# A two-layer MoE with a mixer between, on one core: the slot table from one-hot products and row gathers per expert, in place of zeroed, scattered and reloaded rows

## The chip, the core and the metric

The kernel runs on one core of a Trainium2 chip. Times are device microseconds (us) of one execution. The core's engines are named as the profile names them: PE is TensorE's matmuls, PEld its weight loads, DVE VectorE, ACT ScalarE, POOL GpSimd, SP SyncE, which here only issues transfers. "Granted clock" is the share of TensorE's full clock that the chip allowed in a stretch.

## What is computed

The input x is 2 x 1024 tokens of 512 values, float32. Three stages each add to it: a sparse feed-forward layer with 8 experts, a mixer, and the same feed-forward layer again. Every stage works on the layer-normalized x.

```python
x = x + 0.5 * ffn(layernorm(x), gate_weight, wi, wo)
x = x + mixer(layernorm(x), Wu, bu, Wv, bv, Wg1, bg1, Wg2, bg2, conv_w, conv_b)
x = x + 0.5 * ffn(layernorm(x), gate_weight, wi, wo)

def ffn(inputs, gate_weight, wi, wo):          # T = 2048 tokens, E = 8, C = 320
    logits = tokens @ gate_weight.T
    probs = softmax(logits)
    top1 = argmax(logits)
    mask = one_hot(top1, E)
    ranks = cumsum(mask, axis=0) - 1
    mask = mask * (ranks < C)
    weight = mask * probs                       # at the chosen expert
    dispatch = einsum('tec,th->ech', sec_mask, tokens)
    hmid = gelu(einsum('ech,ehi->eci', dispatch, wi))      # wi 8 x 512 x 2048
    eout = einsum('eci,eih->ech', hmid, wo)                # wo 8 x 2048 x 512
    return einsum('tec,ech->th', combine_weights, eout)
```

So a token goes to its best expert only, in the order of the tokens, and the 321st and later tokens of an expert are dropped. The mixer is a depthwise convolution over three tokens, two projections u and v gated by a small two-step network, a running sum of u over a sequence, and a product with Wu's transpose.

## The kernel before

Tokens lie on SBUF's 128 partitions in 16 tiles, worked on in 4 groups of 4 tiles. Products of float32 are made as three products of rounded halves: a high and a low half of each operand (names ending in h and l), which gives lines L1062 to L1064 (first product of an expert) and L1069 to L1071 (second).

**Routing.** For each group: DVE takes mean and variance (L742 to L749), POOL the power -0.5 (L433) and the shift (L435), ACT normalizes four tiles (L527; of the first group DVE does two, L755), PE turns them (L1099), ACT copies the turned blocks (L537), and PE multiplies by the gate's columns, four accumulating matmuls with 8 columns of weights (L1114). DVE copies the 8x512 result (`lgT`, L772), PE turns it back (L1121), and `route` on DVE finds the best expert, its one-hot row and the exponentials' sum; PE counts the ranks with triangular and all-one matrices (L1134 to L1137). `route(g)` works on the choice of group g and on the ranks of group g-1 in one round of about 20 small operations. Its result is `to_row`, the row of each token in a table in HBM.

**The table `disp`.** It has 2560 slots of 516 values. SP writes zeros over it (L318, four transfers of 1287.5 KB), POOL writes each slot's own number into the last column (L461, 2560 elements of four bytes), and once a group's `to_row` is known and the zeros lie, POOL scatters the normalized tiles with weight, deviation, mean and token number as four further columns, one indirect transfer per tile (L456, 16 per layer). When all have landed, SP loads expert 0's slots (L332, L334) into `dtok`.

**An expert.** PE turns `dtok` (L1160), ACT and DVE split it into high and low half (L583, L734). `wi` and `wo` come in four 1 MB units each, loaded two ahead by SP, split by ACT (L565, L576) and DVE (L734). The hidden layer goes through gelu (L596). ACT restores the unnormalized rows `xr` from `dtok` (L624), DVE copies weight and token number (L922, L923), multiplies and adds (L939), and POOL scatters three parts of up to 128 rows to x1 or out (L506). SP loads `dtok` for the next expert after the turning.

**PE's program.** An expert is computed over the width that its number of tokens needs: 240, 256, 272, 288, 304 or 320 columns, each with its own body of instructions, aligned to blocks of 256. `dispatch` compares the number (loaded into a register by L1239, at each expert) with the widths and branches. It is used twice: `visit`, which branches to the last instruction of the body's block and back at once, ahead of the turning, and `run`, which goes to the body. PE, ACT, DVE and POOL run their expert loops as loops on the chip. Before its loop PE waits for the counts, for the pads that DVE wrote, and for the first split weights.

**Between.** After layer 1's experts SP reloads x1 as `xt`; the mixer runs group by group; the normalizing and routing of layer 2 begin among the mixer's last additions. Layer 2's routing then is the same as that of layer 1, without zeros.

The lines that a sentence can't say as well:

```python
for t in range(g * GROUP, (g + 1) * GROUP):
    pool.indirect_dma_start(disp[:, :], bass.IndirectOffsetOnAxis(ap=to_row[:, t:t + 1], axis=0),
                            xn[:, t, :], None).then_inc(s.scattered, 16)
...
sp.wait_ge(s.scattered, 16 * TILES)
sp.wait_ge(s.taken_done, 1)
load_tokens(s, 0)
...
pe.wait_ge(s.taken_done, 1)
pe.wait_ge(pad_set, n + 1)
pe.wait_ge(s.wi_lo, 1)
```

## Time and profile before

| | us |
|---|---|
| median of three runs | 1210.59 |
| the runs' range | 1208.7 to 1220.23 |
| the profiled execution | 1222.94 |
| its span, from first to last instruction | 1221.2 |
| mean granted clock in it | 0.945 |
| PE, DVE, ACT, POOL busy in it | 1069.9, 737.1, 566.7, 127.8 |

The rows further below are of the profiled execution. "x4" is a count of instructions; a duration before it is their sum, or, where they overlap, the time from the first's start to the last's end. In brackets stands how long the engine was idle before, and what ended that; "issue" is a wait for nothing that the profile shows. In the chain of waits a row is a piece of the path that ended last. In the rows of the page on transfers the last number is the median time from issue to landing.

### The profile page before, as it was taken

What the parts mean: (1) busy time and instruction counts of PE and PEld (TensorE: products, weight loads), DVE (VectorE), ACT (ScalarE), POOL (GpSimd) and SP (SyncE); (2) the same over time, 40 slices, a digit from 0 to 9 for tenths busy, and PEclk for the clock granted to TensorE, in tenths of its full rate; (3) what the DMA queues carried; (4) which work ended last, traced back from release to release, by engine and by line L of the source; (5) the groups of instructions that cost most, each with busy time, mean ns of one, the idle gap of its engine ahead of it and who ended that gap; (6) DMA issues with size and microseconds to landing.
All of it is one profiled execution on the core that took longest, in us unless ns stands there. A gap on an engine that the chain in (4) does not pass through costs nothing.

```text
span 1221.2 us, 20880 instructions
## 1 busy us (share of the span) xinstructions
PE 1069.9 (88%) x7658; PEld 989.6 (81%) x7659; DVE 737.1 (60%) x1199; ACT 566.7 (46%) x871; POOL 127.8 (10%) x140
## 2 busy tenths in 40 slices
PE   5469796999999999759999983999999999879895
PEld 2169795999999999747787751899999999879795
DVE  6535453666657667448777764456767677645551
ACT  4335342556555556344334232445556565534341
POOL 3500101010101101100000015001101001010100
PEclk9779898999999999979999996899999999979998
DMA  9775734375554854040000024644557547523420
GB/s 255 241 253 197 284 121 143 119 253 191 193 193 126 281 185 168 24 136 1 1 35 30 6 104 164 238 159 160 203 180 253 193 153 277 205 92 124 160 69 21
DMA packets 90332, 189.08 MB, mean 155 GB/s; under 512 B 4592, under 2 KB 5104, under 8 KB 90224
## 3 DMA queue, kind: packets, MB, share of 16 engines
q1 hardware_dynamic: 84272, 169.50, 41.2%
q0 software_dynamic: 6016, 18.97, 4.1%
q8 instruction: 31, 0.51, 0.2%
q14 instruction: 13, 0.11, 0.0%
HBM read 160.02 MB, written 32.62 MB: 158 GB/s over the span
## 4 chain that ended last, share of the span: by engine, by line
PE 75%; issue 7%; DMA 6%; ACT 4%; DVE 3%; POOL 3%; SPq 1%; DVEq 0%; ACTq 0%; POOLq 0%
PE psH L1062 11%; PE psH L1063 11%; PE psH L1064 11%; PE acc L1069 9%; PE acc L1070 9%; PE acc L1071 9%; DMA raw_wi<-in_wi 4%; PE acc L1062 3%; PE acc L1063 3%; PE acc L1064 3%; POOL disp L456 2%; PE acc L1160 1%; PE psT L1204 1%; PE psH L1160 1%; PE psT L1099 1%
## 5 line engine op out<-in xcount | busy, mean ns | idle before, releaser
L1062 PE MATMUL psH<-dth,wih 128*128 128x240 f32 (+5 forms) x1024 | 298.8, 292 | 11.3 <-issue 9.4
L1069 PE MATMUL acc<-hth,woh 128*128 128x240 f32 (+5 forms) x1024 | 293.9, 287 | 6.3 <-DVE htl L734 6.3
L1063 PE MATMUL psH<-dtl,wih 128*128 128x240 f32 (+5 forms) x1024 | 297.2, 290 | 0.0
L1064 PE MATMUL psH<-dth,wil 128*128 128x240 f32 (+5 forms) x1024 | 296.8, 290 | 0.0
L1070 PE MATMUL acc<-htl,woh 128*128 128x240 f32 (+5 forms) x1024 | 293.3, 286 | 0.0
L1071 PE MATMUL acc<-hth,wol 128*128 128x240 f32 (+5 forms) x1024 | 293.1, 286 | 0.0
L734 DVE TENSOR_TENSOR wol<-raw_wo,woh 128x1024 fp32r<-128x1024 f32 x128 | 156.4, 1223 | 134.4 <-ACT woh L576 134.3
L1062 PEld LDWEIGHTS psH<-dth,wih 128*128 128x128 f32 x1024 | 196.9, 192 | 15.1 <-issue 13.7
L596 ACT ACTIVATE gel<-psH 128x320 f32<-128x320 f32 x256 | 111.0, 437 | 202.3 <-PE psH L1064 199.1
L576 ACT ACTIVATE woh<-raw_wo 128x1024 fp32r<-128x1024 f32 x128 | 135.4, 1059 | 146.1 <-PE acc L1071 144.4
L1069 PEld LDWEIGHTS acc<-hth,woh 128*128 128x128 f32 x1024 | 193.0, 188 | 7.9 <-DVE htl L734 7.9
L1063 PEld LDWEIGHTS psH<-dtl,wih 128*128 128x128 f32 x1024 | 196.9, 192 | 0.0
L1064 PEld LDWEIGHTS psH<-dth,wil 128*128 128x128 f32 x1024 | 196.7, 192 | 0.0
L1070 PEld LDWEIGHTS acc<-htl,woh 128*128 128x128 f32 x1024 | 193.0, 189 | 0.0
L1071 PEld LDWEIGHTS acc<-hth,wol 128*128 128x128 f32 x1024 | 193.0, 188 | 0.0
L734 DVE TENSOR_TENSOR wil<-raw_wi,wih 128x1024 fp32r<-128x1024 f32 x128 | 155.8, 1219 | 14.3 <-ACT wih L565 14.3
L565 ACT ACTIVATE wih<-raw_wi 128x1024 fp32r<-128x1024 f32 x128 | 134.8, 1054 | 18.5 <-DMA raw_wi<-in_wi 18.5
L891 DVE CAST hth<-gel 128x640 fp32r<-128x640 f32 x128 | 64.9, 507 | 114.1 <-ACT gel L596 114.0
L734 DVE TENSOR_TENSOR htl<-gel,hth 128x640 fp32r<-128x640 f32 x128 | 105.7, 826 | 4.4
L506 POOL DMA_INDIRECT out_x<-eotok,res_row x24 | 36.6, 1525 | 419.9 <-DVE eotok L939 415.0
L506 POOL DMA_INDIRECT x<-eotok,res_row x24 | 36.5, 1520 | 416.2 <-DVE eotok L939 411.3
L1160 PE MATMUL acc<-ident,dtok 128*128 128x128 f32 x96 | 17.8, 336 | 69.8 <-DMA dtok<-disp 40.2
(161 smaller groups left out, 1182.0 us busy)
## 6 DMA issues: line engine op xcount, KB each, us to landing
raw_wi<-in_wi SPq DMA_DIRECT2D x64, 1024.0 KB, 6.7
raw_wo<-in_wo SPq DMA_DIRECT2D x64, 1024.0 KB, 7.5
dtok<-disp SPq DMA_DIRECT2D x16, 516.0 KB, 3.9
disp<-zeros SPq DMA_DIRECT2D x4, 1287.5 KB, 22.2
out_x<-xt SPq DMA_DIRECT2D x4, 1024.0 KB, 4.6
xt<-in_x SPq DMA_DIRECT2D x3, 1024.0 KB, 13.5
xt<-x SPq DMA_DIRECT2D x3, 1024.0 KB, 12.8
dtok<-disp SPq DMA_DIRECT2D x16, 129.0 KB, 4.3
```

What stands on the lines that cost most here:

```text
L506: pool.indirect_dma_start(target[:, :], bass.IndirectOffsetOnAxis(ap=res_row[0:m, k:k + 1], axis=0), eotok[0:m, k, :], None).then_inc(s.re ...
L565: act.activation(wih[:, step % 2, :, :], raw_wi[k][:, :, (step % 2) * HALF:(step % 2 + 1) * HALF], copy).then_inc(s.wi_hi, 1)
L576: act.activation(woh[:, step % 2, :, :], raw_wo[k][:, (step % 2) * ICS:(step % 2 + 1) * ICS, :], copy).then_inc(s.wo_hi, 1)
L596: act.activation(gel[:, step % 2, j, :], psH[j][:, 0:CAP], ACT.Gelu).then_inc(s.gelu_done, 1)
L734: return dve.tensor_tensor(out, full, hi.bitcast(F32), ALU.subtract)
L891: dve.tensor_copy(hth[:, k, :, :], gel[:, k, :, :]).then_inc(s.ht_hi, 1)
L1062: pe.matmul(out, lh, rh, start=first, stop=False)
L1063: pe.matmul(out, lh, rl, start=False, stop=False)
L1064: return pe.matmul(out, ll, rh, start=False, stop=last)
L1069: pe.matmul(out, lh, rh, start=False, stop=False, skip_group_check=True)
L1070: pe.matmul(out, lh, rl, start=False, stop=False, skip_group_check=True)
L1071: return pe.matmul(out, ll, rh, start=False, stop=False, skip_group_check=True)
```

## The change

- The table in HBM, its zeros, its number column, the 16 scatters and the loads of `dtok` are gone. Each token's place (expert, part of 128 slots, lane) is written as one-hot rows: `at_lane` (128 lanes), `at_place` (24 parts), and `at_facts`, the latter times the token's four facts (its number plus one, weight, 1/deviation, shift). `tabulate` sums over the 16 tiles of tokens with one matmul each of 128x128 by 128x96 (L1220 after) into one PSUM bank: the table of slots. DVE's `tables` makes from it the row numbers to read (`src`) and to write (`dst`; empty slots write to rows of their own behind the output).
- POOL gathers an expert's three parts of 128 rows straight from x, in layer 2 from out, into `rows` (two buffers, L451 after); experts 0 and 1 ahead of the loop, e+2 when the three scatters of e have landed. ACT normalizes them into `dn` (`norm_rows`), three operations during the expert before. DVE's `stage`, at the second of its four rounds, waits for the three gathers and copies `dst_now`, `facts_now` and `src_now`. DVE's last operation writes in place of the gathered rows, and POOL scatters from there.
- Routing goes in two batches of eight tiles: `choose` (best expert), `place` (rank, part, lane, the one-hot rows). POOL makes half of each batch's `at_facts`.
- The gate's matmuls go to four column strips of PE (`tile_position`), each for one block of 128 input values; the four partial sums are added by a matmul with `fold`, which also turns them.
- POOL normalizes two tiles of groups 1 to 3 in layer 1, and of the last group in layer 2.
- PE reads the eight counts once, before the loop, into eight registers, and moves them down by one after each expert. ACT's, DVE's and POOL's loops hold two experts per round, the last two stand behind it.
- In layer 2 `logits` and `logits_by_tokens` of groups 0 and 1 and the turning of group 2 stand among the mixer's last matmuls. The last output group is stored before the first weights are loaded. The start of `wo` no longer waits for scatters.

```diff
-            sp.wait_ge(dve_const, 1)
-            for k in range(4):
-                rows = SLOTS // 4
-                sp.dma_start(disp[k * rows:(k + 1) * rows, 0:TOKEN_COL].rearrange("(p r) d -> p r d", p=P),
-                             zeros[:, :].rearrange("p (r d) -> p r d", d=TOKEN_COL)).then_inc(zero_out, 16)
...
-                sp.wait_ge(s.scattered, 16 * TILES)
-                sp.wait_ge(s.taken_done, 1)
-                load_tokens(s, 0)
...
+            def norm(g, s):
+
+                pool.wait_ge(s.var_done, g + 1)
+                pool.wait_ge(s.rstd_done, 2 * g + 1)
+                for t in range(g * GROUP + GROUP // 2, (g + 1) * GROUP):
+                    ins = pool.tensor_scalar(xn[:, t, :], xt[:, t, :], mv[:, t, 0:1], rstd[:, t:t + 1],
+                                             ALU.subtract, ALU.mult)
+                ins.then_inc(s.xn_pool, 1)
...
+            def gather(e, a, source, s):
+
+                pool.wait_ge(s.src_set, e + 1)
+                pool.sem_inc(may_send, 1)
+                for k in range(CHUNKS):
+                    pool.indirect_dma_start(rows[a][:, k, :], None, source,
+                                            bass.IndirectOffsetOnAxis(ap=src_now[:, a, k:k + 1], axis=0)
+                                            ).then_inc(gathered[a][k], 16)
...
+                    if more:
+                        pool.wait_ge(s.res_out, 48 * e + 48)
+                        gather(e + 2, a, source, s)
...
-                    for c in range(DC):
-                        ins = pe.matmul(ps_logitT[g % 2], small[:, GATE0 + c * E:GATE0 + (c + 1) * E],
-                                        xTt[:, g % 2, c, :], start=(c == 0), stop=(c == DC - 1))
+                        pe.wait_ge(s.lgT_copied, g - 1)
+                    for c in range(DC):
+                        strip = slice(c * STRIP, (c + 1) * STRIP)
+                        ins = pe.matmul(ps_logitT[g % 2][strip, :], gates[:, c, :], xTt[:, g % 2, c, :],
+                                        start=True, stop=True, tile_position=(0, c * STRIP))
...
+                def tabulate(b, s=s):
+
+                    for t in range(TB):
...
+                        ins = pe.matmul(psH[0][:, 0:Q * FACTS], at_lane[:, t, :],
+                                        at_facts[:, t].rearrange("p f q -> p (f q)"),
+                                        start=(b == 0 and t == 0), stop=(b == BATCHES - 1 and t == TB - 1))
...
                 pe.wait_ge(s.taken_done, 1)
-                pe.wait_ge(pad_set, n + 1)
                 pe.wait_ge(s.wi_lo, 1)
+                for k in range(E):
+                    pe.reg_load(counts[k], taken[0:1, k:k + 1])
                 pe.reg_mov(later, 0)
                 with pe.Fori(0, E) as e:
-                    pe.reg_load(tokens, taken[0:1, bass.ds(e, 1)])
                     top_bb = nc.cur_bb
                     dispatch("visit")
                     nc.switch_bb(f"visited_{n}", parent=top_bb)
-                    pe.wait_ge(s.dtok_in, 32 * e + 32)
+                    pe.wait_ge(s.dn_done, CHUNKS * e + CHUNKS)
...
+                    for k in range(E - 1):
+                        pe.reg_mov(counts[k], counts[k + 1])
```

PE's order at the end of layer 1's routing and at the loop's start, before (`taken` holds the experts' counts, `ohb` the one-hot choice, `before` the counts so far; TENSOR_LOAD is a load into a register):

```order
L1137 MATMUL acc<-before,ones 128x32
L1154 MATMUL acc<-before,ones 128x8
L1238 UNCONDITIONAL_BRANCH
L1238 ISA
L1239 TENSOR_LOAD taken
L1224 UNCONDITIONAL_BRANCH
L1228 COMPARE_AND_BRANCH x5
L1232 UNCONDITIONAL_BRANCH
L1243 ISA
L1246 REGISTER_ALU
L1160 MATMUL acc<-ident,dtok 128x128 x3
```

and after:

```order
L1201 MATMUL psH<-before,ones 128x64
L1208 MATMUL acc<-before,ones 128x8
L1220 MATMUL psH<-at_facts,at_lane 128x96 x8
L1325 TENSOR_LOAD taken x8
L1327 UNCONDITIONAL_BRANCH
L1312 UNCONDITIONAL_BRANCH
L1316 COMPARE_AND_BRANCH x5
L1320 UNCONDITIONAL_BRANCH
L1331 ISA
L1334 ISA
L1248 MATMUL acc<-ident,dn 128x128 x3
```

Eight matmuls of the second batch's table stand ahead of the loop, and the register's load has moved out of the loop and is there eight times.

POOL's order in layer 1, from the last group's powers to the expert loop, before:

```order
L433 TENSOR_TENSOR rstd<-var,expo 128x4
L435 TENSOR_TENSOR shift<-neg_mean,rstd 128x4
L441 TENSOR_TENSOR xn<-var,rstd 128x4
L442 COPY xn<-mv 128x4
L456 DMA disp<-xn,to_row 4608x516 x16
L512 UNCONDITIONAL_BRANCH
L512 ISA
L504 ISA
L506 DMA x<-eotok,res_row 4608x512
```

and after (`rows_99` and `rows_100` are the two buffers `rows`):

```order
L424 TENSOR_TENSOR facts<-var,expo 128x4
L426 TENSOR_TENSOR facts<-neg_mean,facts 128x4
L433 TENSOR_SCALAR xn<-xt,mv,facts 128x512 x2
L442 TENSOR_TENSOR at_facts<-at_place,facts 128x384 x2
L451 DMA rows_99<-in_x,src_now 128x512 x3
L451 DMA rows_100<-in_x,src_now 128x512 x3
L504 UNCONDITIONAL_BRANCH
L504 ISA
L497 DMA x<-rows_99,dst_now 4608x512
```

Two wide normalizing operations, half of the one-hot facts and six gathers stand where two small columns and 16 scatters stood.

DVE's order in layer 1, after `ranks` of the second batch, after the change (before, two small rounds of `route` stood here, with `pads` and six fills of PSUM banks behind them):

```order
L819 SCALAR_TENSOR_TENSOR t_125<-t_125 128x8
L826 TENSOR_TENSOR at_place<-places,t_125 128x192
L830 TENSOR_TENSOR at_lane<-lanes,t_125 128x512 x2
L835 TENSOR_TENSOR at_facts<-at_place,facts 128x384
L846 TENSOR_SCALAR src_now<-psH 128x3
L848 TENSOR_SCALAR src_now<-psH 128x3
L850 COPY table<-psH 128x96
L852 COPY facts_now<-table 128x12
L853 TENSOR_SCALAR src<-table 128x24
L854 SCALAR_TENSOR_TENSOR away<-table,trash 128x24
L856 SCALAR_TENSOR_TENSOR away<-table,away 128x24
L858 TENSOR_TENSOR dst<-away,trash 128x24
```

and what ended the routing there before:

```order
L811 TENSOR_TENSOR t_122<-t_122 128x4
L816 TENSOR_TENSOR to_row<-t_122,spare 128x4
L852 MEMSET dtok 64x512
L830 CAST taken<-acc 128x8
L858 MEMSET acc 128x512 x4
L858 MEMSET psH 128x512 x2
L734 TENSOR_TENSOR wil<-raw_wi_80,wih 128x1024 x2
```

The wide one-hot operations and the table's eight small ones now stand between the ranks and the first split of weights; the fills have moved to the program's start, for 320 columns of four banks.

## Rows read from the trace of the kernel before

**Rows 1.** Windows by stage: stretch, its length, busy time (instructions) of each engine, clock, DMA share, GB/s.

```profile
0.00:74.30 74.30, 32.68 (x149) 15.69 (x150) 38.22 (x153) 26.46 (x43) 26.53 (x48) 0.80 0.86 247
74.30:510.50 436.20, 411.00 (x3280) 405.58 (x3280) 267.95 (x345) 226.85 (x348) 33.67 (x21) 0.97 0.52 182
510.50:530.00 19.50, 0.85 (x4) 0.85 (x5) 6.48 (x15) 1.52 (x2) 5.65 (x9) 0.63 0.67 167
530.00:720.00 190.00, 182.38 (x831) 143.74 (x830) 137.12 (x238) 76.56 (x118) 8.21 (x18) 0.98 0.07 26
720.00:769.20 49.20, 24.37 (x118) 10.68 (x116) 23.80 (x112) 14.43 (x25) 17.15 (x20) 0.75 0.52 186
769.20:1207.00 437.80, 418.57 (x3280) 413.02 (x3280) 261.44 (x335) 220.83 (x337) 33.78 (x21) 0.97 0.48 167
```

**Rows 2.** The chain of waits in layer 1's routing: start, duration, what.

```profile
41.46 1.10 POOL disp L456
...
61.95 2.94 DMA disp<-xn,to_row
...
65.32 4.08 DMA dtok<-disp
```

**Rows 3.** Timeline of PE, layer 2's first expert: start, duration, operation, idle before.

```profile
764.04 1.54 PE L1160 MATMUL acc<-ident,dtok 128*128 128x128 f32 x6 [17.45 <-DMA dtok<-disp]
```

**Rows 4.** The page's issues of transfers: KB of each, median us to landing.

```profile
disp<-zeros SPq DMA_DIRECT2D x4, 1287.5 KB, 22.2
...
xt<-in_x SPq DMA_DIRECT2D x3, 1024.0 KB, 13.5
...
out_x<-eotok,res_row POOLq DMA_INDIRECT x24, 5.4
...
disp<-slot_rows POOLq DMA_DIRECT2D x2, 10.0 KB, 10.9
```

**Rows 5.** Timeline of DVE and POOL in layer 1's routing.

```profile
14.28 2.47 DVE L742 BATCH_NORM_STATS2 stats<-xt 128x6 f32<-128x512 f32 x4 [3.37 <-DMA xt<-in_x]
...
28.79 0.68 DVE L772 COPY lgT<-acc 8x512 f32<-8x512 f32 x1 [1.41 <-PE acc L1114]
...
2.96 1.46 POOL L461 DMA_DIRECT2D disp<-slot_rows  x1 [0.21 <-issue]
...
8.81 1.05 POOL L433 TENSOR_TENSOR rstd<-var,expo 128x4 f32<-128x4 f32 x1 [4.39 <-DVE var L749]
```

**Rows 6.** Timeline of PE: the gate's matmuls of groups 0 and 1.

```profile
16.21 5.83 PE L1114 MATMUL acc<-xTt,small 128*8 128x512 f32 x8 [0.69 <-ACT xTt L537]
...
25.15 3.60 PE L1114 MATMUL acc<-xTt,small 128*8 128x512 f32 x8
```

**Rows 7.** What ended PE's idle time before L1160; PE's timeline; the page's instruction queue.

```profile
  issue: 28.7, 5
...
210.50 0.39 PE L1062 MATMUL psH<-dth,wih 128*128 128x272 f32 x1 [2.59 <-issue]
...
311.80 0.40 PE L1062 MATMUL psH<-dth,wih 128*128 128x288 f32 x1 [0.61 <-issue]
...
q8 instruction: 31, 0.51, 0.2%
```

**Rows 8.** Timeline of POOL, ACT and DVE within layer 2's second expert.

```profile
833.01 2.41 POOL L506 DMA_INDIRECT out_x<-eotok,res_row  x1 [77.29 <-DVE eotok L939]
...
836.99 1.56 POOL L506 DMA_INDIRECT out_x<-eotok,res_row  x1 [0.30 <-issue]
...
849.19 0.81 ACT L624 ACTIVATE xr<-dtok 128x512 f32<-128x512 f32 x1
...
850.88 0.16 DVE L922 COPY slot_w<-dtok 128x2 f32<-128x2 f32 x1
...
851.69 1.23 DVE L734 TENSOR_TENSOR wol<-raw_wo,woh 128x1024 fp32r<-128x1024 f32 x1 [0.47 <-ACT woh L576]
...
854.63 0.44 ACT L596 ACTIVATE gel<-psH 128x320 f32<-128x320 f32 x1 [0.28 <-PE psH L1064]
```

More of the change, by code:

```diff
@@ L476, in _ @@
                         power(g, s.var_done, s.rstd_done)
-                        columns(g, s)
-                    for g in range(GROUPS):
-                        scatter(g, s)
+                        if g == 0:
+                            pool.sem_inc(s.xn_pool, 1)
+                        else:
+                            norm(g, s)
                 else:
@@ L516, in _ @@
+                with pool.Fori(0, E // 2 - 1) as h:
+                    for a in range(2):
+                        expert(2 * h + a, a, True)
+                for a in range(2):
+                    expert(E - 2 + a, a, False)
         @block.scalar
@@ L1010, in tap @@
                 def tap(g, k):
-                    q = place(g) + k - 1
+                    q = column(g) + k - 1
                     if k == 0:
```

604 lines of the change are left out of this document (338 added, 266 removed).

## Prediction

> **What bounds the kernel now.** I read the windows by stage first [rows 1]. The two expert stages take 436.2 and 437.8 us and hold TensorE (PE) busy for 411.00 and 418.57 of them; the mixer takes 190.0 with 182.38 busy. The change leaves their matmuls alone. What it can give back stands in the two routing stages, 74.3 us with 32.68 busy and 49.2 with 24.37 busy, and in the 19.5 us between experts and mixer with 0.85 busy: 143 us, of which PE works 58.
>
> Next, the chain through routing 1 [rows 2]. The first row scatter starts at 41.46, the sixteenth at 61.95, its data lie in HBM 2.94 later, and expert 0's rows are loaded back in 4.08 more. So 16 scatters cost (61.95-41.46)/15 = 1.37 us each, the round trip through HBM from first scatter to loaded tokens is 28 us, and the first expert matmul comes at 74.3. In layer 2 PE waits 17.45 us for the same load [rows 3], up to 764.04; there PE's last routing work ended at 746.6, and the first expert matmul comes at 769.2. From rows loaded to that matmul it is 74.3-69.4 = 4.9 us, and 769.2-764.0 = 5.2.
>
> The zeroing of 5 MB takes 22.2 us per transfer to land, the column of slot numbers 10.9 us for 10 KB [rows 4]. The column stands at 2.96 in POOL's order, ahead of the input's groups: DVE waits 3.37 us for group 1, until 14.28; from there on four tiles' statistics, 2.47 us, and their few followers set the pace [rows 5].
>
> **The change, part by part.** *Start of layer 1.* Without the 2,560 small elements and the zeros on the rings, group 1 should land where the transfers' rate puts it. The three 1 MB groups, issued together, take 13.5 us to land [rows 4]; at the 247 GB/s of this stage [rows 1] 1 MB takes 4.2 us, so after the first four tiles (1 MB in all, issued from 2.7 on and so landed at about 7) group 1 lands at 11.2. The stage's mean holds its own waits too, so I take 10.5, nearly 4 us sooner than now; the ends are 0 and 4.5.
>
> *Norms and logits.* ACT normalizes two tiles of a group instead of four, POOL the other two. POOL has no 128x512 arithmetic in the trace. Its nearest row is a power of 128x4 in 1.05 us; DVE goes over 128x512 in 0.62 for statistics (2.47 for four) and 0.68 for a copy, ACT in 0.81 [rows 5, 8]. I take 1.0 us a tile, between 0.6 and, at three times DVE's time, 1.9. The four logit matmuls of a group took 3.60 us, at a slower clock 5.83 [rows 6]. Now they go to four different column strips and no longer add up; I take an overlap, 1.0 us at full clock and 1.8 below it. If nothing overlaps they still cost 3.60 and 5.83; the lower end is a single one's time, 0.9. The copy of their result to SBUF keeps its 0.68 (128 partitions instead of 8).
>
> The Trainium skill (TensorE: Matmul & The Clock Gate, Measured speedup vs the span model) lists three column tiles as 2.38 times faster than one after the other. By it 3.60 us would be at most 1.5, half a microsecond above my term; no row of this kernel shows such tiles.
>
> *Routing in two batches.* Before: four rounds of some 20 small DVE operations of 0.14 to 0.21 us, like the copy of 0.16 [rows 8], with a new one every 0.11. After: two rounds with 64 or 8 columns, about 9 operations each (choose, 2.3 us with its waits between engines) and 9 more (place, 1.5 us up to the wide ones). Then, per batch, one 128x192 comparison (about 0.4 by the 128x512 copy's 0.68), two 128x512 comparisons (1.35), one 128x384 product (0.56) and on POOL the same product; then 8 matmuls of 128x96. My order by hand, adding row by row: last group's variance at 27.3, last transpose copied at 34.5, first batch ranked at 35.6 and placed at 39.5, fourth group turned at 40.7, second batch ranked at 44.3 and placed at 48.4, table summed at 50.5. Layer 2 has logits 0 and 1 and two turnings already within the mixer (2.3 us more there); its table is summed at 745.2, 1.4 us before PE's routing work ended until now.
>
> *From the table to the first expert.* Removed: scatters, zeros, two loads. Added are two paths. The rows: 0.3 us DVE, three gathers at 1.37 plus once 1.1 for a neighbour on the port (a scatter beside a weight split takes 2.41 [rows 8]), landing 2.9 after the last issue, normalizing 0.8 [rows 8]: 50.5+0.3+5.2+2.9+0.8 = 59.7. PE's own path: it waits until DVE has written the tables (9 small operations, 1.9) and split the first weights (1.23 [rows 8]), 53.6. Then 8 register loads, of which the profile shows none (I take the 0.4 us of a DMA issue like SP's, 3.2 in all; ends 0.8 and 6), the branches, and the fetch of a body's code that has not been visited. Before, that fetch lies within the wait for the loaded rows (17.45 us in layer 2), a cover that goes; at expert borders such waits last 2.59 us and, over five of them, 5.7 on average [rows 7]. I take 4 us, giving 61.2; the bounds are 0 and 9. With the 4.9 us of before, the first matmul comes at 66.1 instead of 74.3: **-8.2**. Layer 2, likewise from 745.2: tables and split 748.3, loads, branches and code 756.0, plus 5.2 = 761.2: **-8.0**. PE's own path decides in both, the rows have 1.5 to 3 us of slack.
>
> *Between experts and mixer.* The column of layer 2 goes too. It is issued among the reloads of x1 that end this stage's wait; I take **-2.1**, about half of what the first one cost, between 0 and -4.
>
> *Expert loop.* ACT's norm of three gathered parts replaces three residual parts, of the same 128x512; DVE has three small copies where it had four. Gather e+2 may be issued only when the three scatters of expert e have landed. In layer 2's expert 1 the first starts at 833.01 and the last at 836.99 [rows 8] and land 5.4 later [rows 4], 842.4. The gathers then issue until 846.5, with a splitting DVE on the shared port, and land at 849.4 to 851. DVE asks for them where it now copies the weights, at 850.88; ACT next, for a gelu at 854.63. So I take 0, with 3 us of slack; the other bound is +2 per expert beyond it.
>
> *Sum.* -8.2-8.0-2.1 = -18.3. The profiled execution took 1222.94 us (span 1221.2, 1.74 around it), so 1204.6 in its frame. It lies 1.0% above the median 1210.59 of the three runs; taking the difference over, the median becomes 1192.3.
>
> **A rule that speaks against it.** The row: of the 14 borders between two experts, PE's first matmul waits at five for something that the profile doesn't show as a semaphore, 28.7 us in all; the first matmul of 272 columns, at 210.50, adds 2.59 [rows 7]. They stand at some changes of width, whose code has not run for long or never, and not at others: at 311.80 the width goes to 288 with only 0.61. These are fetches of PE's program: the instruction queue carried 31 packets, 0.51 MB, some 16 KB each, the 256 instructions at which the bodies are aligned. After the change the loop's head, which stood within one such block, lies across two, in both layers, since eight loads stand before it and seven register moves behind. Head plus body are then three blocks instead of two.
>
> The Trainium skill (Runtime: NRT & Kernel Launch, Instruction fetch mechanics) says that only two 16 KB lines are held, and that a taken branch to anything else waits for a fetch. By that, every expert would now wait twice. The trace does not bear it out: a change of width with 0.61 us would not be possible, and nine of the 14 borders show no wait.
>
> **The rivals.** *A, code fetches at every expert.* The third block pushes out the body, and each border waits for a fetch of 3 us (the smallest seen is 2.59) more than it does now: 14 borders give +42 (the first expert of each layer is counted above), and 1192+42 = 1234. It decides from 1.3 us a border, where the 18.3 are used up. For it: the split head, and the rule. Against it: nine borders without a wait, several widths held at once in layer 1, and a head that asks for the body's block ahead of the turning of tokens.
>
> *B, gathers too late.* They land over 3 us behind DVE's question. With 12 of 16 experts waiting 2.5 us beyond the slack, +30: 1222. It decides from 1.5 us. For it: scatters in the loop take 1.56 to 2.41 each beside DVE's splits. Against it: loads of weights leave half the rings free (share 0.48 to 0.52).
>
> *C, the head of the chain is dear.* The strips don't overlap, the clock stays at the level of 0.75 to 0.80 [rows 1], POOL needs 1.9 us a tile: +2.6 x 2, +1.8 x 2 on the chain in layer 1, half in layer 2; +13 of the 18 is given back: 1205.
>
> *D, less code to wait for.* The eight loads ahead of the loop and the prefetch of the first body cost nothing, and the visits fall better: 8 to 15 us less, 1177 to 1184.
>
> **How the numbers follow.** Forecast 0.45 (own range 1186 to 1200), D 0.10, C 0.22, A 0.16, B 0.07. A measurement of this kernel tells about 1% from no change: faster is below 1198.5, slower above 1222.7. Faster: 0.44 + 0.10 + 0.04 of C = 0.58; same: 0.01 + 0.18 + 0.06 of A and B, 0.25; slower: 0.17. The range starts at 1174, below D, and ends at 1226, with B and the lighter half of A inside.
>
> **What would show it.** Right: the first expert matmul at about 66 and, with the mixer 2 us earlier and 2 longer, 8 us less in layer 2; PE's wait before L1248 at the loop's start released by no DMA but by DVE or "issue"; expert stages within 3 us of 436 and 438; group 1 of x in DVE's row by 11. Wrong, A: the "issue" gaps at L1248 and L1062 number over ten. Wrong, B: ACT's or DVE's idle time "<-DMA rows", and PE waiting for dn. Wrong, C: logit rows of 3.6 us or more, POOL's norms near 2 us each.

## The result and the profile after

The changed kernel takes 1247.62 us, median of four runs (1239.62 to 1255.49), against 1215.41 for the kernel before in the same comparison: 1.0277 times as long (95% interval 1.0218 to 1.0336), slower by 32 us. The forecast was 1192.3 with a range of 1174 to 1226. The profiled execution took 1248.31 us, with a span of 1246.5. The profiled execution of the kernel before took 1222.94, 7.5 us above that kernel's median here and 13.9 above its median beside the first experiments (1209.09). So its stages are together about 1% longer than usual, and a comparison by stages flatters the other kernels by about that much.

The windows by stage, cut at the same events as [rows 1] (first expert matmul, PE's last matmul of the stage, 0.9 us into the mixer and 190 us on):

```profile
core 0: us, PE busy (x) PEld busy (x) DVE busy (x) ACT busy (x) POOL busy (x), PEclk, DMA share, GB/s
0.00:81.20 81.20, 38.42 (x196) 29.60 (x196) 37.68 (x118) 26.44 (x39) 28.82 (x37) 0.71 0.41 139
81.20:538.40 457.20, 418.05 (x3280) 413.69 (x3280) 265.04 (x331) 223.65 (x343) 54.47 (x39) 0.94 0.50 171
538.40:557.30 18.90, 0.87 (x4) 0.87 (x5) 6.48 (x15) 1.52 (x2) 4.19 (x7) 0.61 0.64 228
557.30:747.30 190.00, 182.07 (x843) 143.85 (x842) 139.22 (x241) 76.32 (x118) 7.29 (x12) 0.98 0.05 20
747.30:801.90 54.60, 24.26 (x152) 20.16 (x151) 24.08 (x74) 15.71 (x24) 13.69 (x12) 0.66 0.44 152
801.90:1233.30 431.40, 415.48 (x3280) 411.11 (x3280) 258.55 (x321) 215.44 (x333) 54.34 (x39) 0.98 0.49 165
```

Taken from the stages of before, that is +6.9 us in routing 1, **+21.0 in the first expert stage**, -0.6 between experts and mixer, +5.4 from the mixer to layer 2's first expert matmul, and -6.4 in the second expert stage: +26.3, and 1.0 less behind the last matmul, which makes the 25.3 us between the spans, where the medians are 32 apart. The stages that were to give 18 us back cost 11.7 (+6.9-0.6+5.4); the stage that was to change by nothing cost 21. Where that went shows at the borders between experts.

A border is the step from one expert's last product to the next one's first. Experts count from 0; layer 1's have 288, 304, 272, 240, 288, 240, 240 and 256 columns, layer 2's 320, five times 240, and twice 320. PE's timeline of layer 1, the turning of the next expert's rows (L1248) and the first matmul behind it (L1119); in brackets the idle time before and what ended it:

```profile
139.83 1.54 PE L1248 MATMUL acc<-ident,dn 128*128 128x128 f32 x6 [6.04 <-issue]
...
206.55 1.54 PE L1248 MATMUL acc<-ident,dn 128*128 128x128 f32 x6 [8.95 <-issue]
...
264.93 1.54 PE L1248 MATMUL acc<-ident,dn 128*128 128x128 f32 x6 [4.98 <-issue]
...
273.05 0.56 PE L1119 MATMUL psH<-dth,wih 128*128 128x240 f32 x1 [2.87 <-issue]
...
323.43 1.53 PE L1248 MATMUL acc<-ident,dn 128*128 128x128 f32 x6 [5.57 <-issue]
...
331.12 0.60 PE L1119 MATMUL psH<-dth,wih 128*128 128x288 f32 x1 [2.79 <-issue]
```

The first two waits were there before, at 134.99 and 202.40, with 7.85 and 9.08 us (and 2.59 behind the second). The others are new: the borders to experts 3, 4 and 5 had no wait for more than 0.61 us [rows 7]; now they have 4.98+2.87, 5.57+2.79 and, at 387.80 and 394.92, 4.41+2.02, together 22.6 us. The page's instruction queue answers to them: 43 packets where there were 31.

```profile
q8 instruction: 43, 0.70, 0.3%
```

In layer 1's routing the timelines of POOL and PE show what the estimates of the parts became:

```profile
14.60 4.14 POOL L433 TENSOR_SCALAR xn<-xt,mv,facts 128x512 f32<-128x512 f32 x2
...
31.30 4.13 POOL L433 TENSOR_SCALAR xn<-xt,mv,facts 128x512 f32<-128x512 f32 x2
...
31.35 1.07 PE L1176 MATMUL acc<-xTt,gates 128*32 128x512 f32 x8
...
35.53 3.74 PE L1159 MATMUL psT<-ident,xn 128*128 128x128 f32 x16 [3.12 <-issue]
...
54.98 3.70 PE L1220 MATMUL psH<-at_facts,at_lane 128*128 128x96 f32 x16 [3.32 <-POOL at_facts L442]
```

POOL needs 2.07 us a tile, twice the estimate and above its upper bound of 1.9. PE starts the last turning at 35.53, 0.1 us after POOL is done (31.30+4.13=35.43; the profile calls the releaser "issue", so that POOL holds it up is read from the times). The strips overlap as assumed: 1.07 us at full clock and 1.94 at half, where [rows 6] had 3.60 and 5.83. The table is summed at 58.7 instead of 50.5. The chain from there to the first expert, start, duration and piece:

```profile
61.38 1.99 POOL rows L451
63.38 0.30 issue
63.68 5.94 DMA rows<-in_x,src_now
...
69.70 0.82 ACT dn L586
70.52 1.72 issue
72.25 1.54 PE acc L1248 x6
...
76.07 5.12 issue
81.18 0.60 PE psH L1119
```

The third gather lands 5.94 us after its issue, not 2.9. The rows are ready at 70.5, PE 1.7 us later, and between the turning and the first matmul stands a second wait of 5.12. PE's own branch instructions show what it does meanwhile: a COMPARE_BRANCH at 65.3 lasts 6.16 us and one at 76.5 lasts 4.15, where the median one takes 0.07.

### The profile page after: what moved, and what is told of

It is laid out like the page before. It is cut to its first block, busy times and chain, and to the rows that moved or that the text cites. A ratio compares the mean times of both kernels' runs of the same rounds, so it can differ in the third digit from the quotient of the medians.

```text
span 1246.5 us, 20666 instructions
## 1 busy us (share of the span) xinstructions
PE 1079.2 (87%) x7750; PEld 1019.3 (82%) x7750; DVE 733.1 (59%) x1102; ACT 559.1 (45%) x859; POOL 165.6 (13%) x149
## 4 chain that ended last, share of the span: by engine, by line
PE 76%; issue 8%; DMA 4%; DVE 2%; ACT 2%; POOL 2%; POOLq 0%; DVEq 0%; SPq 0%; ACTq 0%
PE psH L1119 11%; PE psH L1120 11%; PE psH L1121 11%; PE acc L1127 9%; PE acc L1128 9%; PE acc L1126 9%; PE acc L1119 3%; PE acc L1121 3%; PE acc L1120 3%; DMA rows<-out_x,src_now 2%; PE acc L1248 1%; PE psT L1292 1%; PE psH L1248 1%; DMA rows<-in_x,src_now 1%; POOL rows L451 1%
## 5 line engine op out<-in xcount | busy, mean ns | idle before, releaser
L1119 PE MATMUL psH<-dth,wih 128*128 128x240 f32 (+5 forms) x1024 | 300.8, 294 | 30.9 <-issue 28.3
L1126 PE MATMUL acc<-hth,woh 128*128 128x240 f32 (+5 forms) x1024 | 293.1, 286 | 0.0
L1119 PEld LDWEIGHTS psH<-dth,wih 128*128 128x128 f32 x1024 | 198.1, 193 | 35.1 <-issue 32.1
L1126 PEld LDWEIGHTS acc<-hth,woh 128*128 128x128 f32 x1024 | 193.0, 188 | 0.0
L497 POOL DMA_INDIRECT x<-rows,dst_now x24 | 36.0, 1498 | 386.5 <-DVE rows L987 381.6
L497 POOL DMA_INDIRECT out_x<-rows,dst_now x24 | 35.8, 1493 | 363.3 <-DVE rows L987 358.4
L1248 PE MATMUL acc<-ident,dn 128*128 128x128 f32 x96 | 19.1, 354 | 62.0 <-issue 62.0
## 6 DMA issues: line engine op xcount, KB each, us to landing
raw_u<-in_wuT SPq DMA_DIRECT2D x1, 1024.0 KB, 11.5
```

Source lines behind the costliest of these rows:

```text
L497: pool.indirect_dma_start(target[:, :], bass.IndirectOffsetOnAxis(ap=dst_now[0:m, a, k:k + 1], axis=0), rows[a][0:m, k, :], None).then_inc ...
L1119: pe.matmul(out, lh, rh, start=first, stop=False)
L1126: pe.matmul(out, lh, rh, start=False, stop=False, skip_group_check=True)
```

## The experiments

Each run has the kernel before beside it on the same chip; its median there was 1209.09 beside the whole head, the kernel before with a split head, the five widths and the first run on DVE's order; 1211.75 beside the second run on DVE's order, ACT's norms, the early counts and the held loads; 1209.43 beside the four edits together and the first two runs of three widths; 1214.36 beside the four widths and the last three runs. "Block" is 256 instructions of PE's program, the unit to which the bodies are aligned; where the head lies is read from the built program.

**One alignment ahead of the loop.** The loop then holds its head in one block, six bodies and the tail: 8 blocks instead of 9.

```diff
+                pe.addr_align(BLOCK, offset=0, max_nops=0)
                 pe.reg_mov(later, 0)
                 with pe.Fori(0, E) as e:
```

> The changed kernel with one alignment ahead of each expert loop, so that the loop's head lies in one block of 256 instructions; the loop then spans 8 blocks (head, six bodies, tail) instead of 9. Theory 1 (PE holds about 8 blocks, a ninth throws out what the next expert needs): the waits for 'issue' at the borders to layer 1's experts 3, 4 and 5, 22.6 us together in the changed kernel, fall to under 4, expert stage 1 comes back from 457 to about 435, time about 1222 instead of 1247.6. Theory 2 (a split head costs at every expert, whatever else): the same here. Rival (the waits belong to the changed registers and moves, or come by chance of addresses): stage 1 stays within 5 us of 457 and the time over 1240.

Measured: 1205.44 us, 0.9967 of before (0.9924 to 1.001). One line of alignment takes 42 us off (two other kernels with a split head, timed beside it, took 1247.35 and 1250.05), more than both theories asked. The same borders, and the windows of the expert stages:

```profile
254.74 0.82 PE L1248 MATMUL acc<-ident,dn 128*128 128x128 f32 x6
...
258.04 0.37 PE L1119 MATMUL psH<-dth,wih 128*128 128x240 f32 x1 [0.23 <-issue]
...
301.55 0.87 PE L1248 MATMUL acc<-ident,dn 128*128 128x128 f32 x6 [0.37 <-issue]
...
305.18 0.39 PE L1119 MATMUL psH<-dth,wih 128*128 128x288 f32 x1 [0.52 <-issue]
```

```profile
76.90:499.90 423.00, 405.42 (x3280) 401.29 (x3280) 266.59 (x333) 223.08 (x344) 54.99 (x39) 0.98 0.54 185
...
760.20:1190.90 430.70, 416.27 (x3280) 412.01 (x3280) 259.99 (x323) 216.26 (x333) 56.04 (x39) 0.98 0.49 166
```

The first expert stage falls from 457.2 to 423.0. Of these 34.2 us, 12.6 are PE's busy time for the same 3280 matmuls (418.05 to 405.42): after a wait the granted clock is lower for a while, as the six turnings of 1.54 us at half clock against 0.82 show. Against the 22.6 us of waits, that is about half again their length.

**The kernel before with its head over two blocks.** No other instruction changes.

```diff
+                pe.addr_align(BLOCK, offset=200, max_nops=0)
                 pe.reg_mov(later, 0)
                 with pe.Fori(0, E) as e:
```

> The kernel before with an alignment that puts its loop's head over two blocks (9 blocks in the loop instead of 8); nothing else changes. Theories 1 and 2: waits for 'issue' appear at the borders to layer 1's experts 3 to 5 as in the changed kernel, expert stage 1 grows from 436 to 453 to 458, time about 1232 to 1238. Rival (registers and moves of the change are the cause): within 4 us of before.

Measured: 1262.57 us, 1.0409 of before (1.0318 to 1.0499), 53 us slower. The borders that the change had spoilt are spoilt here too, without any of the change:

```profile
268.62 1.54 PE L1160 MATMUL acc<-ident,dtok 128*128 128x128 f32 x6 [4.92 <-issue]
...
323.61 1.54 PE L1160 MATMUL acc<-ident,dtok 128*128 128x128 f32 x6 [6.41 <-issue]
...
331.64 0.60 PE L1062 MATMUL psH<-dth,wih 128*128 128x288 f32 x1 [3.63 <-issue]
```

So the registers and moves are not the cause, except that they moved the head. The size was underrated again.

That these idle times are waits for code, which "issue" doesn't say, can be read from two views of the stretch that holds the borders to experts 3, 4 and 5: PE's branch instructions in `dispatch` (durations in ns: least, median, longest) and the packets of the instruction queue. In order: before, the change, the change with the whole head, before with the split head.

```profile
L1228 PEldq COMPARE_BRANCH  x12: 64/142/325, 259.3 to 364.9; - x12
L1316 PEldq COMPARE_BRANCH  x12: 64/1662/5427, 258.6 to 391.1; - x12
L1316 PEldq COMPARE_BRANCH  x12: 64/142/328, 253.5 to 358.3; - x12
L1228 PEldq COMPARE_BRANCH  x12: 64/151/6002, 262.7 to 393.2; - x12
```

```profile
q8 instruction: 2, 0.03, 0.1%
q8 instruction: 11, 0.18, 0.5%
q8 instruction: 2, 0.03, 0.1%
q8 instruction: 8, 0.13, 0.4%
```

The same 12 branches take at most 0.33 us in the first and third kernel; in the second and fourth the longest take 5.4 and 6.0, and PE's program is fetched: 11 and 8 packets against 2.

**Fewer widths, head over two blocks.** Is it the number of blocks, or the split? Three runs take bodies away and hold the head over two blocks; a fourth has the head whole. Experts whose width is gone are computed over the next one.

```diff
-WIDTHS = range(240, CAP + 1, 16)
+WIDTHS = [240, 272, 288, 304, 320]
...
+                pe.addr_align(BLOCK, offset=200, max_nops=0)
```

> The changed kernel with the width 256 left out (layer 1's last expert is computed over 272 columns, +3 us) and its head held over two blocks: 8 blocks in the loop, head still split. Theory 1 (number of blocks): no waits at the borders to layer 1's experts 3 to 5, stage 1 at about 438, time 1225 to 1230. Theory 2 (the split head itself): the waits stay, stage 1 at about 460, time 1245 to 1252.

> The changed kernel with four widths (240, 272, 288, 320), head over two blocks: 7 blocks. If 8 blocks hold (the loop's 7 and the one behind it that is fetched ahead), no waits over 2 us at the borders to layer 1's experts 4 and 5; stage 1 about 440. If fewer hold, waits of 4 to 8 us there as with five widths; stage 1 about 460.

> The changed kernel with three widths (240, 288, 320) and the head held over two blocks: 6 blocks in the loop. Three experts of layer 1 are computed over wider columns (+12 us). Theory 1 in its first form (the number of the loop's blocks against about 8): no waits for 'issue' over 2 us at the borders to layer 1's experts 3 to 5, whose widths 240, 288, 240 have all but one run before. Theory 3 (a border touches head, second head block, old body, tail, new body and the blocks behind them; what is not of the last border or two is gone): waits of 4 to 8 us at each of these borders as in the changed kernel.

> The same three widths with the head in one block: 5 blocks in the loop. All theories: no waits over 2 us at the borders to layer 1's experts 3 to 5, expert stage 1 shorter than in the run with the split head by 0 to 3 us (theory 1) or by 15 to 25 us (theory 3).

Measured with five widths (8 blocks): 1250.05 us, 1.03 (1.0219 to 1.0382), the waits as before. With four (7 blocks): 1252.69, one run, and still the waits. With three (6 blocks): 1215.09, one run, and in layer 1 they are gone, also at the border to expert 2, but not in layer 2:

```profile
324.57 1.54 PE L1248 MATMUL acc<-ident,dn 128*128 128x128 f32 x6 [5.62 <-issue]
...
332.30 0.40 PE L1119 MATMUL psH<-dth,wih 128*128 128x288 f32 x1 [2.30 <-issue]
```

```profile
201.48 0.82 PE L1248 MATMUL acc<-ident,dn 128*128 128x128 f32 x6
...
255.46 0.82 PE L1248 MATMUL acc<-ident,dn 128*128 128x128 f32 x6
...
302.24 0.87 PE L1248 MATMUL acc<-ident,dn 128*128 128x128 f32 x6
...
356.27 0.81 PE L1248 MATMUL acc<-ident,dn 128*128 128x128 f32 x6
...
1140.57 0.63 PE L1119 MATMUL psH<-dth,wih 128*128 128x320 f32 x1 [3.71 <-issue]
```

The first block above is of four widths, the second of three; its last row is layer 2's expert 7, whose 320 columns are also those of expert 6. With three widths and a whole head (5 blocks) one run took 1194.54. Its first expert stage, 422.2 us, is 2.6 shorter than with the split head (the "0 to 3" of theory 1); of the 20.5 us between the two runs 5 stand before layer 1's first expert matmul, 6.4 before layer 2's and 7 in the second expert stage, 3.7 of them the row above.

My first theory, a fixed room of eight blocks, fell with the five and the four widths; the second, that a split head costs at every expert, and the third, that nothing older than a border or two is kept, fell with the three widths. One border fits none of them: layer 2's expert 6 needs the 320 columns that expert 0 had, five experts of 240 lie between, and PE waits in every kernel here, even with 5 blocks in the loop and a whole head:

```profile
1052.03 1.54 PE L1248 MATMUL acc<-ident,dn 128*128 128x128 f32 x6 [5.28 <-issue]
```

What the runs show is narrower than a rule: at layer 1's borders to experts 3, 4 and 5 the waits stand with a split head at 7, 8 and 9 blocks and not at 6, and with a whole head not at 8. The three widths don't test much there, as these experts go between 240 and 288 alone, whose bodies then lie side by side. Which blocks PE gives up for a new one stays open.

**Order of DVE's statistics.** In the change DVE copies group 0's logits before it takes group 2's statistics; it waits 4.00 and 4.78 us there.

```diff
-                    moments(1, s.var_done, [x_in[0]] * GROUP)
+                    for g in range(1, GROUPS):
+                        moments(g, s.var_done, [x_in[g - 1]] * GROUP)
...
                     lgT_copy(0, s)
-                    moments(2, s.var_done, [x_in[1]] * GROUP)
                     lgT_copy(1, s)
-                    moments(3, s.var_done, [x_in[2]] * GROUP)
```

> The changed kernel with DVE's statistics of layer 1's groups 1 to 3 ahead of the copies of the first two logits, as the order was before. Theory (DVE waits for the logits, 4.0 and 4.8 us, and by that holds up the statistics, POOL's norms and PE's turnings of the next groups): the last turning starts at 29 to 31 instead of 35.5, the first expert matmul at 74 to 77 instead of 81.2, time 4 to 7 us less, 1241 to 1244. Rival (POOL's two norms of 4.1 us set the pace): POOL's chain 14.4 + 3 x 5.4 gives 30.6 at the earliest, and what PE gains there is lost in waiting for the code of the loop: first matmul within 1.5 us of 81.2.

> On the kernel with the whole head (1205.4 us; first expert matmul at 76.9): DVE's statistics of layer 1's groups 1 to 3 ahead of the copies of the first logits. Theory (the order on DVE holds up the chain of the next groups): the first expert matmul 4 to 6 us earlier, 71 to 73, and the whole 4 to 6 us less, about 1200. Rival (the gain is lost again before the end, as the run on the split head with 1247.35 against 1247.62 reads): time within 1.5 us of 1205.4.

Measured on the split head: first expert matmul at 77.27, 3.9 us earlier, though the input came 2.2 us later in that execution; time 1247.35, 1.0274 (1.0188 to 1.0359), nothing to be seen. On the whole head: first matmul at 70.3, 6.6 us earlier; 1201.85 us, 0.9925 (0.9879 to 0.9971). The term is confirmed in the profile, as kernels with a whole head that change nothing in layer 1's routing have their first matmul at 75.2 to 76.9; the time is 3.6 us lower, within the intervals.

**ACT's norms again.**

```diff
-                        norm(g, s.rstd_done, s.xn_done, GROUP // 2)
+                        norm(g, s.rstd_done, s.xn_done, GROUP if g else GROUP // 2)
...
-                for t in range(g * GROUP + GROUP // 2, (g + 1) * GROUP):
-                    ins = pool.tensor_scalar(xn[:, t, :], xt[:, t, :], mv[:, t, 0:1], rstd[:, t:t + 1],
-                                             ALU.subtract, ALU.mult)
-                ins.then_inc(s.xn_pool, 1)
+                pool.sem_inc(s.xn_pool, 1)
```

In layer 2 the last group's norms change in the same way.

> On the kernel with the whole head: ACT normalizes all four tiles again (groups 1 to 3 of layer 1, the last of layer 2), POOL none; DVE still takes half of group 0. Theory (POOL's two norms of 4.14 us are 1.2 us slower than ACT's four of 2.94): 1.2 us off each of three groups in layer 1 and off one in layer 2, first expert matmul at 73.3 instead of 76.9, time 4 to 5 us less. Rival (ACT's copies of turned tokens then wait behind the norms): within 1 us.

Measured: first expert matmul at 73.5, 3.4 us earlier, as worked out; 1195.75 us, 0.9876 (0.984 to 0.9913). POOL's help with the norms was a loss. The time fell by 9.7 us where the theory asked for 4 to 5; the rest is not traced, and such a difference proves little by itself (see the held loads below).

**Counts and first code earlier.**

```diff
                 take_counts()
+                pe.wait_ge(s.taken_done, 1)
+                for k in range(E):
+                    pe.reg_load(counts[k], taken[0:1, k:k + 1])
                 tabulate(1)
...
-                pe.wait_ge(s.taken_done, 1)
-                pe.wait_ge(s.wi_lo, 1)
-                for k in range(E):
-                    pe.reg_load(counts[k], taken[0:1, k:k + 1])
...
+                    pe.wait_ge(s.wi_lo, 1)
                     pe.wait_ge(s.dn_done, CHUNKS * e + CHUNKS)
```

> On the kernel with the whole head: PE loads the eight counts ahead of the second batch's table products, where it waits 3.3 us anyway, and no longer waits for the first split weights before it asks for the body's code. Theory (in layer 2 PE's own path of loads and code fetch ends 3.4 us after the rows are normalized at 751.5; in layer 1 1.3 us after 70.7): 1 to 1.5 us in layer 1 and 3 to 3.5 in layer 2, 4 to 5 us together. Rival (the fetch collides with the gathers then and both end as late as now): under 1.5 us together.

Measured: first matmul at 76.3 (0.6 us earlier); in layer 2 it comes 240.2 us after the mixer's start instead of 242.5, 2.3 us less. 1202.4 us, 0.9908 (0.9862 to 0.9953). That is at most three of the 4 to 5 us expected, and neither part is clear of noise: two kernels whose routing in layer 2 is unchanged show 240.2 and 240.9 there. The row that the theory is about did change: with the code there in time, the rows become the last (the gathers land 6.7 and 6.1 us after issue).

**Loads held back for the gathers.**

```diff
                     done = e * STEPS + 2 * (k + 1)
+                    sp.wait_ge(s.dn_done, CHUNKS)
                     sp.wait_ge(s.wi_lo, done)
```

> On the kernel with the whole head: SP issues its third unit of weights only when expert 0's rows are normalized. Theory (the 1 MB load issued at 62.6 makes the second and third gather land after 7.0 and 6.6 us instead of 3.7): they land within 4.5 us, the rows of layer 1 are normalized by 68.5 instead of 70.75; PE's own path, at 72.0, hides nearly all of it, 0 to 1.5 us less. Rival (the gathers are slow of themselves, 128 descriptors each on one queue): landing as before, time the same or, for late weights, 1 to 3 us more.

Measured: second and third gather land 4.4 and 4.5 us after issue instead of 7.0 and 6.6, so 2.6 and 2.1 us of that are the 1 MB load beside them. The first matmul is not earlier (77.3). The time, 1197.64 us, 0.9861 (0.9815 to 0.9907), is 7.8 us under the whole head alone, whose interval begins at 0.9924, where the theory allowed 1.5 at most. The profile shows another place for it, the last two borders of layer 2, where PE waited 5.46, 2.95 and 5.22 us with the whole head alone. Here it waits 5.46 before expert 6's turning, and of expert 7's border only 0.97 us are left, before its first product:

```profile
1122.45 0.83 PE L1249 MATMUL acc<-ident,dn 128*128 128x128 f32 x6
```

The second expert stage is 420.1 us long instead of 430.7. PE's program is the same in both kernels, so which fetches it waits for there does not follow from the program alone; what decides it stays open. The second run on DVE's order shows the same (418.7 us), those with ACT's norms, the early counts and the four edits don't. Differences of up to 10 us between kernels with a whole head can come from these borders.

**The four together.**

> The kernel with the whole head and all four later edits together: statistics first, ACT's norms, counts early, loads of weights held until expert 0's rows are normalized. Theory (the edits shorten different pieces of the same chain): first expert matmul at 66 to 69 instead of 76.9, and 3 to 6 us less in layer 2's routing, time 1186 to 1194, 1.5 to 2% under before. Rival (one of them already takes what the others would, and the rest is noise of the runs): not under 1195.

Measured: first matmul at 70.67; in layer 2 237.2 us after the mixer's start instead of 242.5. 1194.57 us, 0.9867 (0.9816 to 0.9919), under the rival's bound by less than the noise, and no lower than ACT's norms (1195.75) or the held loads (1197.64) alone within their intervals. That the four gains add up is not shown in the time. The profile's routing is 11.5 us shorter than with the whole head alone, yet its execution only 1.1: 10 us come back in the two expert stages. 3.8 of them stand at the border to expert 2, where this execution waits for code between the turning and the first matmul (8.1 us from the one to the other against 4.35); the rest is spread, and I have not traced it.

**The change where code costs little.** Three widths and a whole head, in the kernel before and in the changed one; then with the four edits.

```diff
-WIDTHS = range(240, CAP + 1, 16)
+WIDTHS = [240, 288, 320]
```

> The kernel before with the three widths (head whole in both layers): the waits at the borders to layer 1's experts 2 and layer 2's expert 7 go (17 and 5 us), three experts are 10 us longer: 1198 to 1204 by theory 3 (fetches belong to the number of blocks, in the kernel before too). Rival (fetches there are first visits that stay): 1215 to 1222.

> The changed kernel with three widths and a whole head once more, timed beside the kernel before with three widths: the difference is the worth of the change itself. By the prediction's sum 18 us; by the stages of the run with the whole head (routing +2.6 and +2.5, expert loop 1 us less for each of 14 experts) 8 to 12 us under that kernel.

> Whole head, the four edits on routing, and three widths (240, 288, 320). Against the kernel with the whole head alone: 6 us from the earlier first matmul of layer 1, 5 from layer 2's routing, 11 from missing fetches less wider columns (the one run of three widths with a whole head took 1194.5). Theory (the parts add up): 1181 to 1187, under all kernels so far. Rival (1190 to 1195 is what is left whatever is mended, since the clock falls after each wait): 1190 or more.

Measured: the kernel before with three widths 1202.22 us, 0.9908 (0.9877 to 0.994); the changed kernel so 1198.7, 0.9871 (0.9842 to 0.99). The waits at the borders to layer 1's expert 2 and layer 2's expert 7 are gone in the kernel before too, as theory 3 had it there, and its time is within that theory's range. The difference between the two kernels, 3.5 us, is the worth of the change itself, not the 18 of the forecast and not the 8 to 12 expected here; the intervals overlap, so even its sign is not sure. With the four edits 1187.66 us, 0.9801 (0.9775 to 0.9827): 2% under the kernel before, the best of all, and 0.7 above the theory's range. Its stages, from an execution of 1182.7, 5 us under that median:

```profile
0.00:67.60 67.60, 31.96 (x196) 25.77 (x196) 35.67 (x117) 29.59 (x45) 15.38 (x31) 0.75 0.47 159
67.60:487.90 420.30, 413.46 (x3280) 409.31 (x3280) 266.31 (x333) 222.56 (x344) 58.05 (x39) 0.99 0.54 187
...
696.90:742.60 45.70, 26.14 (x153) 21.30 (x151) 22.07 (x73) 16.78 (x26) 9.53 (x10) 0.62 0.51 163
742.60:1167.70 425.10, 415.32 (x3280) 410.73 (x3280) 260.04 (x323) 215.78 (x334) 55.11 (x39) 0.98 0.48 169
```

Here PE works 8 us longer in stage 1 than with the whole head alone, on wider columns, and the stage is 2.7 us shorter all the same.

## Why the prediction was wrong

**The step that failed is the expert loop, "So I take 0", and with it the weight of rival A.** The rival named the place (the head over two blocks), the sign and the threshold, and I gave it 0.16. I set against it nine borders without a wait and several widths held at once. That says only "there is room"; how much room was left was never bounded. One reading was wrong: the five waits do not all stand at changes of width. The last is at a border from 320 to 320 columns, so a width that had run just before did not keep PE from waiting. I would now take that as a sign that room was short; with three widths this wait is gone:

```profile
1144.15 1.54 PE L1160 MATMUL acc<-ident,dtok 128*128 128x128 f32 x6 [5.27 <-issue]
```

The price, 3 us at each of 14 borders, was wrong in shape: it is 6 to 8 us at three borders, to 240 columns that had not run yet in this layer, to 288 that had, and back to 240; 22.6 us of waits, with the slower clock behind each. The other borders changed little. Together with the waits in the head of each layer's first expert, the alignment alone is worth 42 us, which happens to be the rival's sum. The sign named for A, over ten "issue" gaps, was no sign, for the kernel before has 14 of them (5 and 9); their length tells, 38.1 us before and 90.3 after, those at each layer's first expert included.

**With the whole head the forecast would have looked right, by luck.** That kernel's profiled execution, 1205.94, is 1.3 us from the 1204.6 of the sum in the same frame. Its two routings and the mixer's start are 22.5 us dearer than forecast (+4.2 for -18.3), and its expert stages 20.3 us shorter than the 0 forecast.

**Routing 1, -8.2 forecast, +6.9 measured.** The table came 8.2 us late, from two terms above all: POOL's tiles at 2.07 instead of 1.0 us, outside the bounds (worth 3.4 us by the run with ACT's norms), and the order by hand did not put enough weight on DVE's wait for logits before the statistics (6.6 us by the run that undoes it; the two overlap). From table to first matmul it is 22.5 us instead of 15.6, by two waits for code: the first of 6.2 rather than 4, and a second in the head, which the whole head takes away (9 us from turning to first matmul become 4.7). The gathers landed after 6 to 7 us rather than 2.9, but the rows were still ready 1.7 us before PE; they count only once PE's own path is shorter. Right were the input (DVE starts group 1 at 9.96; forecast 10.5), the strips, and the eight register loads, 3.0 us against 3.2. The last was luck: the prediction says that the profile shows none, yet the trace of before has 16, of 0.30 to 0.50 us.

**Layer 2, -8.0 forecast, +5.4 measured:** 6.3 us of the miss stand between the table and the first matmul, where the two waits for code are; the table is 7.1 us later after the mixer's start than forecast, and no run takes that apart. With all four edits and three widths the stage is 3.5 us shorter than before (45.7 to 49.2).

**Between experts and mixer, -2.1 forecast, -0.6 measured.** The groups of x1 land after 9.8 us by the page instead of 12.8, but PE starts on the first tiles, which gained little (3.1 us instead of 3.6).

**A gain that I did not see.** In the kernel before PE waits at the second product for DVE's low half of the hidden layer, in the changed one never:

```profile
  DVE htl L734: 6.3, 7
```

That is the row of before, what ended PE's idle time before L1069; the same line after, L1126, has no such row. With the whole head an expert of 240 columns takes 46.4 us from turning to turning in layer 2 (818.13 to 1003.69, four experts), against 47.4 before (828.24 to 1017.71). I read it so that ACT's and DVE's restoring and copying of rows had stood in the way of the last round; no run undoes that part alone. Its size is not pinned: the expert stages of the run with the whole head are 20 us shorter than before, but part of that is the long execution of before and its wait of 2.59 us, and between the two kernels with three widths, whose profiled executions have the same span (1205.3), the expert stages are 6 us shorter and the routing 7 longer.

**Rivals.** C came true as well: the strips overlapped, but POOL took the 2.07 us that C named, and the clock was lower still than C's 0.75 to 0.80, 0.71 in routing 1 and 0.66 in layer 2's; what the clock alone cost is not isolated, and the order on DVE was in no rival. A and C together, with the unseen gain against them, make the result. B's first sign came, its price did not: DVE waits for gathers at six of the 14 borders, 0.9 to 2.6 us each and 10.1 in all, so the slack of 3 us that I took was not there, but PE waits for no rows there, and ACT only at the first expert of a layer. D's hope, a better fall of the visits, came by the alignment and by fewer widths.

On the rule that the prediction weighed: the Trainium skill (Runtime: NRT & Kernel Launch, Instruction fetch mechanics) says that only two lines of 16 KB are kept, and in the same section gives PE 128 KiB, which is eight such lines. The runs agree that a branch to code that is not there costs a fetch: the long branches last 3.1 to 7.4 us here. They don't agree with two lines, since layer 2's experts 2 to 5 of the change go through a head in two blocks, a body and a tail with no wait over 0.2 us before the turning; nor with a plain eight, since the waits stand at seven blocks too.

## What to carry to other kernels

A loop whose bodies are chosen at run time has a working set of code, and its head's place is part of it: look where loop heads fall before and after any edit ahead of them, and fix them with an alignment, as a few instructions more cost 42 us here and one aligned head gave them back. Of bodies specialized by size keep those that pay for their code: three widths beat six here, by 12 us in the kernel before and by 7 in the changed one, though experts compute over wider columns. When a trace shows no wait at most changes of code, look for the one wait that has no reason: it tells how much room is left. And bound an operation that an engine has never run in the trace by more than its neighbour's speed, above all on GpSimd, before it is put on the chain.

## What the runs showed of the hardware that I had not expected

- A wait for code costs more than itself: PE's same 3280 matmuls take 418.05 us with the waits and 405.42 without the new ones, as the granted clock is at its lower level, half of the upper, for a stretch after each (0.94 of full in the stage against 0.98).
- Where the code is not there, the branch instruction itself is long in the trace: 3.1 to 7.4 us instead of 0.07, with packets of the instruction queue beside it. That tells a wait for code from other idle time called "issue".
- GpSimd takes 2.07 us for a 128x512 float32 subtract and multiply, VectorE 0.5 for the same (1.00 for two), ScalarE 0.74 (2.94 for four).
- Four matmuls with 32 weight columns in four column strips take 1.07 us where four accumulating ones with 8 columns took 3.60. The Trainium skill (TensorE: Matmul & The Clock Gate, Measured speedup vs the span model) gives 2.38 for three strips; four give 3.4 here.
- Gathers of 128 rows of 2 KB land 3.7 us after issue alone, 4.4 behind one another, and 5.9 to 7.0 beside a 1 MB load.
